# Batch boundaries zeroed before every scan, one scan over two states, and two VectorE steps moved, in an audio-tower kernel on one Trainium2 core

## The reference

```python
h = tok(x)                                   # patches of 128, hop 64, times W, plus b: (64, 10, 512)
h = h + attn(layernorm(h))
h = h + ffn(layernorm(h))

def attn(x):
    h = x + mamba(rmsnorm(x, rms1_w))
    hn = rmsnorm(h, rms2_w)
    return h + (silu(hn @ gate_w.T) * (hn @ up_w.T)) @ down_w.T

def mamba(x):                                # 64 batches of 10 steps, 1024 channels, 16 states each
    z, xv, B, C, dt_in = split(x @ in_proj_w.T)
    dt = softplus(dt_in @ dt_proj_w.T + dt_proj_b)
    dA = exp(dt * A)                         # A = -exp(A_log)
    dBx = (dt * x_full) * B
    h = 0                                    # for each batch anew
    for t in range(10):
        h = dA[t] * h + dBx[t]
        y[t] = sum over states of C[t] * h
    return ((y + D_skip * x_full) * silu(z)) @ out_proj_w.T

def ffn(x):
    return (silu(x @ w_gate.T) * (x @ w_up.T)) @ w_down.T
```

## Time and profile before

| | us |
|---|---|
| median of 3 runs | 672.27 (670.28 to 673.62) |
| the profiled execution | 675.34 |
| its span, first to last instruction | 673.6 |
| TensorE busy in it | 631.9 |
| VectorE busy | 425.7 |
| ScalarE busy | 328.4 |
| GpSimd busy | 429.1 |

### The profile page before, as it was taken

How to read it: one execution, slowest core, us unless ns; L and a number is a source line. 1 busy time by engine, 2 the same in 40 slices (tenths; PEclk the granted TensorE clock), 3 DMA queues, 4 the chain that set the end, 5 groups by cost and what they waited for, 6 DMA issues and landing times.

```text
span 673.6 us, 8617 instructions
## 1 busy us (share of the span) xinstructions
PE 631.9 (94%) x2846; PEld 505.8 (75%) x2846; DVE 425.7 (63%) x660; ACT 328.4 (49%) x645; POOL 429.1 (64%) x244
## 2 busy tenths in 40 slices
PE   4969998799999989999979999999999999999998
PEld 3736765466665757777747777766999998999998
DVE  4077996889888879889888988851322223332132
ACT  4348788348878263323356323322642442653441
POOL 0176885437786999987877987644455464445461
PEclk9879998799999989999989999999999999999999
DMA  8799997489999959998967999543344343244421
GB/s 325 250 352 377 310 304 274 142 262 352 359 370 353 394 211 353 412 351 323 313 250 264 328 327 314 192 125 120 136 152 126 125 157 126 63 130 131 146 67 44
DMA packets 49164, 163.50 MB, mean 243 GB/s; under 512 B 4320, under 2 KB 18528, under 8 KB 48480
## 3 DMA queue, kind: packets, MB, share of 16 engines
q1 hardware_dynamic: 49120, 162.95, 69.8%
HBM read 145.24 MB, written 17.69 MB: 242 GB/s over the span
## 4 chain that ended last, share of the span: by engine, by line
PE 75%; DVE 13%; ACT 4%; POOL 3%; issue 3%; DMA 2%; SPq 0%; DVEq 0%; ACTq 0%; POOLq 0%
PE work L996 54%; PE da L996 15%; DVE da L787 7%; PE work L1006 5%; DVE hs L798 3%; POOL hs L453 2%; ACT L528 1%; DMA bb<-b_rows 1%; ACT da L551 1%; DMA b_rows<-sq 1%; DMA sm<-small 1%; POOL hs L466 0%; DVE a L853 0%; ACT z L667 0%; DVE work L813 0%
## 5 line engine op out<-in xcount | busy, mean ns | idle before, releaser
L787 DVE TENSOR_TENSOR_SCAN da<-da,hs 128x290 f32<-128x290 f32 (+1 forms) x256 | 198.2, 817 | 35.9 <-POOL hs L453 21.1
L453 POOL TENSOR_TENSOR hs<-dtx,bb 128x1160 f32<-128x1160 f32 (+1 forms) x64 | 171.2, 2676 | 60.8 <-PE work L1006 53.7
L551 ACT ACTIVATE da<-dt,a_neg 128x261 f32<-128x261 f32 (+1 forms) x256 | 118.4, 496 | 141.8 <-DVE hs L798 141.7
L432 POOL TENSOR_TENSOR ws<-wraw,ws 128x1024 fp32r<-128x1024 f32 x40 | 101.5, 2538 | 92.8 <-ACT ws L559 92.8
L996 PE MATMUL work<-sq,wraw 128*128 128x290 f32 x512 | 125.7, 407 | 1.1 <-DVE sq L886 1.1
L996 PE MATMUL work<-hn,win 128*128 128x290 f32 (+1 forms) x336 | 104.5, 459 | 16.3 <-DVE hn L861 8.0
L996 PEld LDWEIGHTS work<-sq,wraw 128*128 128x128 f32 x512 | 96.5, 189 | 30.1 <-issue 1.8
L798 DVE TENSOR_TENSOR hs<-da,cb 128x580 f32<-128x580 f32 (+1 forms) x128 | 105.2, 822 | 10.1 <-DMA cb<-c_rows 3.4
L996 PEld LDWEIGHTS work<-hn,win 128*128 128x128 f32 x336 | 65.5, 200 | 50.6 <-issue 25.7
L559 ACT CAST ws<-wraw 128x1024 fp32r<-128x1024 f32 x48 | 50.3, 1048 | 70.4 <-PE da L996 34.4
L996 PE MATMUL work<-hn,ws 128*128 128x350 f32 x480 | 79.2, 323 | 1.6 <-DVE hn L957 1.6
(11 more groups left out here) (97 smaller groups left out, 630.5 us busy)
## 6 DMA issues: line engine op xcount, KB each, us to landing
wraw<-w_stream SPq DMA_DIRECT2D x104, 512.0 KB, 4.1
bb<-b_rows SPq DMA_DIRECT2D x32, 700.0 KB, 7.3
cb<-c_rows SPq DMA_DIRECT2D x32, 700.0 KB, 5.6
bb<-b_rows SPq DMA_DIRECT2D x32, 580.0 KB, 8.1
cb<-c_rows SPq DMA_DIRECT2D x32, 580.0 KB, 6.0
c_rows<-c_rows SPq DMA_DIRECT2D x8, 875.0 KB, 11.0
c_rows<-c_rows SPq DMA_DIRECT2D x8, 725.0 KB, 6.9
win<-w_in SPq DMA_DIRECT2D x4, 1024.0 KB, 13.8
```

The costliest lines, as they stand in the source:

```text
L432: nc.gpsimd.tensor_tensor(ws[:, k % NW, 1, :], wraw[:, split_loads[k] % NRAW, :], ws[:, k % NW, 0, :].bitcast(F32), ALU.subtract).then_inc ...
L453: nc.gpsimd.tensor_tensor(hs[:, u % NH, 0:NQ * n].rearrange("p (n t) -> p n t", t=n), dtx[:, t % 2, 0:n].unsqueeze(1).to_broadcast([P, NQ, ...
L551: last = nc.scalar.activation(dst, src, ACT.Exp, scale=a_neg[:, j:j + 1])
L787: nc.vector.tensor_tensor_scan(da[:, k % ND, 0:w], da[:, k % ND, 0:w], hs[:, u % NH, p * w:(p + 1) * w], 0.0, ALU.mult, ALU.add).then_inc( ...
```

## The change

`da` becomes two tiles of two banks, one for each half of a unit, with the two states of a half side by side. `decay` writes zeros into the first column of every batch of a half by a ScalarE copy from a small tile `zeros` (58 or 70 columns at a stride of ten), and then the two ACTIVATEs; it counts `da_done` up once a half. `scan` runs once over the two states, so a unit is scan, times_c, scan, times_c. The memset of `da` goes. Two steps move in VectorE's list: the `gate` from the end of the unit with u % 4 = 1 to the middle of the unit with u % 4 = 2, after its first `times_c`; and `("ln1", 1)`, chunk 1's first variance, from slot 15 to the head of slot 16. The schedule, the ring of banks and the other engines' lists are as before.

```diff
 def recurrence(u):
-    return [("scan", u, 0), ("scan", u, 1), ("times_c", u, 0), ("scan", u, 2), ("scan", u, 3), ("times_c", u, 1)]
+    return [("scan", u, 0), ("times_c", u, 0), ("scan", u, 1), ("times_c", u, 1)]
...
+        zeros = sb("zeros", [P, 2 * TM // STEPS])
...
-        da = ctx.enter_context(nc.psum_tensor("da", [P, ND, BANK], F32))
+        da = ctx.enter_context(nc.psum_tensor("da", [P, 2, 2 * BANK], F32))
...
             def decay(u, p):
...
-                if k >= ND:
-                    act.wait_ge(c_times, (k - ND) // 2 + 1)
+                if u >= 1:
+                    act.wait_ge(c_times, 2 * (u - 1) + p // 2 + 1)
...
-                last.then_inc(da_done, 1)
+                if p % 2 == 0:
+                    first = da[:, p // 2, 0:2 * n].rearrange("p (b t) -> p b t", t=STEPS)[:, :, 0]
+                    nc.scalar.copy(first, zeros[:, 0:2 * n // STEPS])
+                dst = da[:, p // 2, p % 2 * n:(p % 2 + 1) * n].rearrange("p (b t) -> p b t", t=STEPS)[:, :, 1:]
+                j = m * NS + q * NQ + p
+                last = nc.scalar.activation(dst, src, ACT.Exp, scale=a_neg[:, j:j + 1])
+                if p % 2 == 1:
+                    last.then_inc(da_done, 1)
...
+            nc.vector.memset(zeros[:, :], 0.0)
             nc.vector.memset(mean_w[:, :], 1.0 / D).then_inc(consts_done, 1)
-            nc.vector.memset(da[:, :, :], 0.0).then_inc(da_zeroed, 1)
...
+            def scan(u, j):
+                w = 2 * TS[u // UNITS]
...
+                dve.wait_ge(da_done, 2 * u + j + 1)
+                nc.vector.tensor_tensor_scan(da[:, j, 0:w], da[:, j, 0:w], hs[:, u % NH, j * w:(j + 1) * w], 0.0,
                                              ALU.mult, ALU.add).then_inc(scan_done, 1)
...
             for i, (unit, steps) in enumerate(late(slots, 1)):
+                steps = [s for s in steps if s != ("ln1", 1)]
+                if i >= 1 and ("ln1", 1) in slots[i - 1][1]:
+                    steps = [("ln1", 1)] + steps
                 parts = []
                 if unit is not None:
                     parts = recurrence(unit)
-                    if unit % QU == 1 and unit > QU:
-                        parts.append(("gate", unit // QU - 1))
+                    if unit % QU == 2 and unit > QU:
+                        parts.insert(2, ("gate", unit // QU - 1))
```

More of the change, by code:

```diff
@@ L35 @@
 BANK = 512
[L37 to L40, removed]
+PRODUCTS = 2 * NCH * UNITS
 IN_DT, IN_X, IN_B, IN_CZ = 0, 1, 3, 5
@@ L72, in unit_of @@
     return u // UNITS, u % UNITS // QU, u % QU
-def piece(u, p):
-    c = u // UNITS
-    return PIECE0[c] + u % UNITS * NP[c] + p
 def products_through(u):
-    return piece(u, NP[u // UNITS] - 1) // 2 + 1
+    return 2 * (u + 1)
 def recurrence(u):
-    return [("scan", u, 0), ("scan", u, 1), ("times_c", u, 0), ("scan", u, 2), ("scan", u, 3), ("times_c", u, 1)]
+    return [("scan", u, 0), ("times_c", u, 0), ("scan", u, 1), ("times_c", u, 1)]
 def m_steps(c):
@@ L247, in build @@
         work = [ctx.enter_context(nc.psum_tensor(f"work{i}", [P, BANK], F32)) for i in range(NG + 1)]
-        da = ctx.enter_context(nc.psum_tensor("da", [P, ND, BANK], F32))
-        banks = [w[:, :] for w in work] + [da[:, i, :] for i in range(ND - 1)]
+        da = ctx.enter_context(nc.psum_tensor("da", [P, 2, 2 * BANK], F32))
+        banks = [w[:, :] for w in work] + [da[:, i // 2, i % 2 * BANK:(i % 2 + 1) * BANK] for i in range(ND - 1)]
         pat_loaded, tokw_loaded, small_loaded = sem("pat_loaded"), sem("tokw_loaded"), sem("small_loaded")
@@ L270, in build @@
         sp_act, sp_small, dt_ready = sem("sp_act"), sem("sp_small"), sem("dt_ready")
-        dtx_done, dbx_done, da_done, da_zeroed = sem("dtx_done"), sem("dbx_done"), sem("da_done"), sem("da_zeroed")
+        dtx_done, dbx_done, da_done = sem("dtx_done"), sem("dbx_done"), sem("da_done")
         scan_done, c_times, th_done = sem("scan_done"), sem("c_times"), sem("th_done")
@@ L539, in decay @@
                 c, m, q = unit_of(u)
-                k, n = piece(u, p), TS[c]
-                if k == 0:
-                    act.wait_ge(da_zeroed, 1)
+                n = TS[c]
+                if (u, p) == (0, 0):
+                    act.wait_ge(consts_done, 1)
                     act.wait_ge(a_neg_done, 1)
                 act.wait_ge(dt_ready, c * KI + m + 1)
-                if k >= ND:
-                    act.wait_ge(c_times, (k - ND) // 2 + 1)
+                if u >= 1:
+                    act.wait_ge(c_times, 2 * (u - 1) + p // 2 + 1)
                 src = dt[:, m, 0:n].rearrange("p (b t) -> p b t", t=STEPS)[:, :, 1:]
[L548 to L551, removed]
-                last.then_inc(da_done, 1)
+                if p % 2 == 0:
[6 more added lines that the diff above has]
+                    last.then_inc(da_done, 1)
             def split_high(k):
@@ L713, in _ @@
                     decay(0, 1)
-                if unit is not None and NP[unit // UNITS] == 4:
+                if unit is not None:
                     decay(unit, 2)
@@ L779, in _ @@
             nc.vector.tensor_scalar(a_neg[:, :], a_neg[:, :], -1.0, None, ALU.mult).then_inc(a_neg_done, 1)
[L781 to L784, removed]
+            def scan(u, j):
+                w = 2 * TS[u // UNITS]
+                if j == 0:
                     dve.wait_ge(dbx_done, u + 1)
-                dve.wait_ge(da_done, k + 1)
-                nc.vector.tensor_tensor_scan(da[:, k % ND, 0:w], da[:, k % ND, 0:w], hs[:, u % NH, p * w:(p + 1) * w], 0.0,
+                dve.wait_ge(da_done, 2 * u + j + 1)
+                nc.vector.tensor_tensor_scan(da[:, j, 0:w], da[:, j, 0:w], hs[:, u % NH, j * w:(j + 1) * w], 0.0,
                                              ALU.mult, ALU.add).then_inc(scan_done, 1)
             def times_c(u, j):
-                c, k = u // UNITS, piece(u, 2 * j)
-                w = GS[c] * TS[c]
-                here = slice(2 * j * w, 2 * (j + 1) * w)
+                w = 2 * TS[u // UNITS]
+                here = slice(j * w, (j + 1) * w)
                 if j == 0:
                     dve.wait_ge(c_loaded[u % NC], 16 * (u // NC + 1))
-                dve.wait_ge(scan_done, k + 2)
-                nc.vector.tensor_tensor(hs[:, u % NH, here].rearrange("p (i w) -> p i w", w=w), da[:, k % ND:k % ND + 2, 0:w],
-                                        cb[:, u % NC, here].rearrange("p (i w) -> p i w", w=w), ALU.mult).then_inc(c_times, 1)
+                dve.wait_ge(scan_done, 2 * u + j + 1)
+                nc.vector.tensor_tensor(hs[:, u % NH, here], da[:, j, 0:w], cb[:, u % NC, here],
+                                        ALU.mult).then_inc(c_times, 1)
             def gate_y(t):
@@ L1017, in keep_clock @@
                 for _ in range(KEEP_CLOCK):
-                    nc.tensor.matmul(da[:, ND - 1, 0:P], mean_w[:, :], mean_w[:, :], start=True, stop=True)
+                    nc.tensor.matmul(da[:, 1, BANK:BANK + P], mean_w[:, :], mean_w[:, :], start=True, stop=True)
             def gate_or_up(s, i):
```

## The result

The changed kernel takes 695.93 us (median; 693.24 to 698.0) against 672.94 for the kernel before beside it: 1.0325 times as long, 95% interval 1.0298 to 1.0351. The forecast was 691.3. The profiled execution of the changed kernel took 695.56 us, its span is 693.8, so the two profiles differ by 20.2 and the two medians by 23.0.

A forecast was written before the change was run, and what follows sets the result against it. TensorE, 94% busy, was taken as the bound. Turn 0.8, bank waits 12.9, low clock 5.4, less 0.1 for the last scan, make 19.0; on 672.27 that gives 691.3 us, range 681 to 697.

The forecast's parts named there:

- The bank of `ysum`: Chunk 1: later gates free this PSUM bank later, so TensorE waits 12.9 us in all, tiles 8 to 14.
- Rival 2: Chunk 1: the bank is free in time as VectorE runs half a unit ahead; 674.2 us, chance 0.09.
- The low clock behind the three long gaps: Chunk 1, tiles 8, 10 and 12: TensorE at 1.2 GHz after each long wait, 3 x 1.8 = 5.4 us.
- Rival 1: Chunk 1: the waits come but the clock doesn't fall after the three gaps; 685.9 us, chance 0.22.
- Chunk 0: a gain: Chunk 0, before its end: a gain of some 2.3 us, bounds 0 and 3.
- `hn` is ready about 2.5 earlier: Unit 15: `mean` after both halves, the second inside VectorE's 4.43 wait, so chunk 1's normed input comes about 2.5 us earlier.
- paying for ScalarE's lateness: Chunk 0: VectorE no longer standing for a tile's last state sum (2.19 us) offsets its added waits for ScalarE.
- The turn: Where chunk 0 ends: first `out` waits for tile 7's gate, the gain is lost; +0.8 us, from -1 to +2.6.
- The merged scan: VectorE: scans of about 1.38 and 1.64 us, saving 0.04 us a half, all beside TensorE's work.
- Rival 4: Merged scans start later and reach the path, VectorE's waits on ScalarE each 0.6 us longer; 677 us, chance 0.04.
- rivals 3 and 4: Rival 3: VectorE is the bound in the recurrence and its saved time reaches the end; 665.0 us, chance 0.05.
- the turn at +2.6 and one more gap at the low clock: Upper end of the range: the worst case where chunk 0 ends plus one further low-clock gap, given as 697 us.

The follow-up runs named there:

- ysum_sbuf: The changed kernel, gates still late, but D*x of chunk 1 written back over xf in SBUF so it takes no PSUM bank: 676.68 us, 1.0041 to the kernel before.
- gate_back_c1: The changed kernel with the gates of tiles 8 to 14 back in their early place, tiles 0 to 7 late: 676.68 us, 1.003 to the kernel before.
- gate_back_c0: The changed kernel with the gates of tiles 0 to 7 back in their early place, tiles 8 to 14 late: 693.07 us, 1.027 to the kernel before.
- before_fill: The kernel before plus 8 and 16 small useless products ahead of those of `rms2` and `ln2_var` in chunk 0: 670.12 us, 0.9953 to the kernel before.
- var_back: The changed kernel with only chunk 1's variance step back in its old place: 695.71 us, 1.0318 to the kernel before.
- merge_only: The kernel before with the merged scan and zero copies alone, gates early and variance in its old place: 675.31 us, 1.0009 to the kernel before.
- gate_back_7: The changed kernel with late gates for tiles 0 to 6 alone, those of tiles 7 to 14 early: 671.26 us, 0.9963 to the kernel before.
- gate_back: The changed kernel with all gates back in their old place, merged scans, zero copies and earlier variance kept: 674.28 us, 1.0004 to the kernel before.
- before_gate_late: The kernel before with the gate's move alone, single scans, memset zeros and variance in its old place: 693.15 us, 1.0278 to the kernel before.
- clock_fill: The changed kernel with one up product of chunk 0 computed twice, just ahead of tile 8's wait: 693.64 us, 1.0284 to the kernel before.

## Why the prediction was right, and where it was off

**The bank of `ysum`** was the term that decided, and each wait came out near its size:

| tile | 8 | 9 | 10 | 11 | 12 | 13 | 14 | sum |
|---|---|---|---|---|---|---|---|---|
| predicted | 3.6 | 0.6 | 3.0 | 1.1 | 3.0 | 1.0 | 0.6 | 12.9 |
| measured | 3.75 | 0.68 | 2.92 | 1.28 | 2.98 | 0.99 | 0.68 | 13.3 |

That was to be had from the trace of before because an order written out by hand has few unknowns: who owns the bank next, when TensorE wants it, and what VectorE now does first. ysum_sbuf shows the mechanism, gate_back_c1 and gate_back_c0 that it is chunk 1's. Rival 2, a bank that is free in time, is refuted by the six stretches.

**The low clock behind the three long gaps** was put at 3 x 1.8 = 5.4; the lengths above give 1.7 + 3.1 + 1.8 = 6.6. The 1.8 was read off eight records against 2.0; at the full clock they take 2.19 (at 240.58) or 2.22 (before_fill), so the price there is 1.6, and behind a longer run of records it is 1.7 to 3.1. Rival 1, that it would not fall, is refuted for these executions, though gate_back_c0 shows that sometimes it doesn't fall.

**Chunk 0: a gain came, but not from the cause given.** The step that failed is "`hn` is ready about 2.5 earlier" because of the variance step. `hn` came 3.6 earlier (0.5 of it because TensorE's first product of the input starts earlier, 5.56 against 6.09), but var_back has that gain without the step. Why the step is worth nothing is seen on VectorE (timeline, kernel after):

```profile
113.88 1.37 DVE L784 TENSOR_TENSOR_SCAN da<-da,hs 128x580 f32<-128x580 f32 x1 [3.93 <-ACT da L548]
...
115.97 2.04 DVE L842 SCALAR_TENSOR_TENSOR h<-a,cols,work 128x350 f32<-128x350 f32 x4
```

The second half in front of `mean` (the last row) now waits 3.93 for ScalarE's `da`, where VectorE stood 4.43 for TensorE before; one wait took the other's place, and `mean` starts at 115.97 in both kernels. In var_back, with one half ahead of it, it starts at 112.64.

The likeliest source of the gain is the late gates. Without them VectorE stands three times or more for a tile's last state sum in chunk 0 (2.19, 1.01 and 1.39 in the kernel before, 1.70, 0.33 and 1.00 in merge_only), the first time ahead of `hn`; in the eight profiles with late gates it does so nowhere for over 0.2 before the gate of tile 7. I had counted this as paying for ScalarE's lateness and no more. From TensorE's first product of the input to `hn` it is 117.8 to 121.1 us in those eight (mean 119.4) and 120.0 to 122.5 in the five without (121.6). The two sets overlap, so 2.2 is known only roughly; gate_back_7 against gate_back, 0.9963 against 1.0004, gives 2.8.

Some of the 3.6 is the clock's. In the profiled execution of the kernel before it was low just ahead of the product that `mean` waits for; in before_fill, the same program up to there, it was not (windows of the kernel before, then of before_fill):

```profile
110.00:114.00 4.00, 3.70 (x8) 2.37 (x9) 1.43 (x3) 3.87 (x9) 0.00 (x0) 0.57 0.95 334
```
```profile
110.00:114.00 4.00, 4.00 (x17) 3.03 (x16) 0.96 (x2) 3.97 (x8) 1.42 (x1) 1.00 0.79 294
```

Before_fill's TensorE was 1.6 ahead in front of these records (108.71 against 110.30) and 2.9 ahead from there to `hn` (125.71 against 128.64): 1.3 us for that stretch. With the 0.5 of the start this leaves some 1.8 of the 3.6 for the gates, an estimate from these single executions.

**The turn.** Predicted was a TensorE that starts 1.5 later after an idle 4.5 (its own terms, 0.45 + 1.5 + 2.3, give 4.25), at the low clock for 1.8. It started 0.3 earlier, after 3.81, and the clock cost 17.58 - 15.89 = 1.7. The mis-sized term is when the DMA of `cb`, the rows of C that `times_c` reads, lands: I moved it by 2.3, it moved by 4.1. The `times_c` behind it started at 220.78 before, and after (VectorE's timeline):

```profile
216.66 0.89 DVE L794 TENSOR_TENSOR hs<-da,cb 128x700 f32<-128x700 f32 x1 [0.90 <-DMA cb<-c_rows]
```

The 2.08 idle before the squares left the clock up, so 1.6 (3.82 - 2.19) of the 1.8 that the prediction named as possible came back: `rms2` ends at 242.8 against 243.9, -1.1 where I had +0.8. The mechanism held: gate_back_c1 and gate_back_7 differ by tile 7's gate alone, and 1.003 against 0.9963 is 4.5 us.

**The merged scan** takes 1366 and 1622 ns; 1.38 and 1.64 were predicted. A zero copy is 211 or 221 ns long, but the ACTIVATE behind it starts after 0.15 (251.31 and 251.47, ScalarE's timeline). Rival 4's condition did come: VectorE's waits on `da` rose from 5.4 to 12.0 us. But merge_only and gate_back, which have them too (8.5 and 11.6), lie at 1.0009 and 1.0004, so neither these waits nor the saved 0.04 a half changes the time beyond the intervals (0.2%), which disposes of rivals 3 and 4. The rule of the Trainium skill that stood beside rival 4 (Perfetto Trace Analysis, Optimizing Scalar/DVE Operations: breaking instructions up may end work sooner) is borne out by no run here.

**The sum.** On the profiles: waits 13.3, clock 6.6, turn -1.1 make 18.8 of the measured 20.2. Both traces hold the same 2846 records of TensorE in the same order, so the rest can be read record by record. Each of the six stretches also costs the 0.16 by which a record otherwise overlaps the next: ahead of tile 8's wait a record starts at 248.63, lasts 0.40, and the next starts 3.75 later, at 252.78, while in the kernel before the same two start 0.24 apart. That is 0.9 in all. The eight records at 362.09 take 4.14 against 3.85, 0.3, and 0.2 is spread over the rest. From 457.08 to the end the two kernels stay 20.2 apart.

That the sum came so near, 19.0 against 20.2, is in part luck: the turn was put 1.9 too high, the clock 1.2, the waits 0.4 and the smaller costs 1.4 too low. So is the range: "the turn at +2.6 and one more gap at the low clock" adds 1.8 + 1.8 to 691.3, which is 694.9 and not the 697 given, and 695.93 lies above 694.9.

On the medians the difference is 23.0, so 2.8 of the 4.6 that the forecast was low come from which executions were profiled, mostly from that of before, 675.34: the median of before was 672.3 in the first runs and 673.8 to 675.2 beside the experiments, a spread nearly as large as what was missed.

## What to carry to other kernels

When a step is moved, list what it releases besides its result: here the gate also freed a PSUM bank that TensorE came round to three products later, and half a unit of delay on an engine with time to spare (VectorE, 61% busy) became 20 us on the one without (TensorE, 92%). Before an engine's waits are made shorter or longer, look at what a gap does to the clock behind it; a gap that must stay can be filled with work of no use. And a gain in one place wants the row of what is late next: by the medians the late gates did bring chunk 0 forward, and a single gate at the turn gave it back.

## What the runs showed of the hardware that was not expected

In these kernels the low clock behind a gap is not fixed by the gap's length. Behind tile 10's stretch of 2.84 to 2.92, in five kernels, the same 56 records took 13.94 (gate_back_c0), 15.56 (before_gate_late), 15.63 (clock_fill), 16.87 (the change) and 16.92 (var_back) us: at 13.8 for full speed, a price between 0.1 and 3.1. Stretches of 1.92 to 2.08 before `rms2` (six kernels in which tile 7's gate is late) were always followed by the full clock, those of 3.27 and more in the rows above never by the full clock throughout. And it can fall behind shorter ones: among the products of `tokc` the kernel before and before_fill stood 1.26 and then 0.87 us alike, and the clock from 110 to 114 was 0.57 in the one and 1.00 in the other. A gap near 3 us is thus priced here by a range, not by a number. And TensorE's useless work was free in a gap: 48 small records in before_fill took 5.7 us and made the kernel 3 us faster.
